# Selective-scan kernel: of every other group of states GpSimd makes both additions, and TensorE adds one product in place of two

## What is computed

```python
dA = jnp.exp(dt_t[..., None] * A)
dBx = dt_t[..., None] * B_t[:, None, :] * x_t[..., None]
h = dA * h + dBx
y = jnp.einsum('bdn,bn->bd', h, C_t)
```

## Time and profile before

| | |
|---|---|
| median of 3 runs | 5212.23 us (5211.99 to 5219.82) |
| the profiled execution | 5224.23 us, its span 5222.4 us |
| TensorE matmuls busy | 4637.5 us, 89% |
| VectorE busy | 4505.1 us, 86% |
| GpSimd busy | 3920.3 us, 75% |
| ScalarE busy | 3588.5 us, 69% |
| mean granted TensorE clock | 0.954 |

### The profile page before, as it was taken

How to read it: one execution, slowest core, us unless ns; L and a number is a source line. 1 busy time by engine, 2 the same in 40 slices (tenths; PEclk the granted TensorE clock), 3 DMA queues, 4 the chain that set the end, 5 groups by cost and what they waited for, 6 DMA issues and landing times.

```text
span 5222.4 us, 73049 instructions
## 1 busy us (share of the span) xinstructions
PE 4637.5 (89%) x22816; PEld 3957.5 (76%) x22816; DVE 4505.1 (86%) x7793; ACT 3588.5 (69%) x8734; POOL 3920.3 (75%) x2218
## 2 busy tenths in 40 slices
PE   5677889989899998989999898999989899998886
PEld 4466777878787787878778787878878787886766
DVE  2598988989899898989989898999989898998950
ACT  2477667777777777777777777777777777776730
POOL 0387777878788787878878787877878787888840
PEclk8788989999999999999999999999999999998998
DMA  4423224343432434343243434324343433433222
GB/s 152 153 83 127 105 89 158 121 156 130 148 132 106 172 115 163 124 153 131 102 172 120 159 123 158 129 102 172 119 161 118 163 123 107 166 106 140 87 94 85
DMA packets 158436, 682.05 MB, mean 131 GB/s; under 512 B 18912, under 2 KB 27744, under 8 KB 108896
## 3 DMA queue, kind: packets, MB, share of 16 engines
q1 hardware_dynamic: 139616, 643.82, 35.0%
q10 hardware_dynamic: 18432, 33.56, 1.7%
HBM read 622.26 MB, written 55.05 MB: 130 GB/s over the span
## 4 chain that ended last, share of the span: by engine, by line
POOL 58%; issue 22%; PE 11%; DVE 4%; DMA 3%; ACT 2%; POOLq 1%; SPq 0%; DVEq 0%; ACTq 0%
POOL dbx L349 36%; POOL half L357 18%; PE gx L521 4%; POOL dtx L392 3%; PE g L554 2%; DVE hb L923 2%; PE g L437 1%; PE ys L447 1%; DMA bb<-bc_scratch 1%; DMA bc_scratch<-ssmT 1%; POOL x L372 1%; DVE gx L977 1%; DVE hc L938 1%; PE gx L486 1%; DMA wf<-wf_scratch 0%
## 5 line engine op out<-in xcount | busy, mean ns | idle before, releaser
L923 DVE TENSOR_TENSOR_SCAN hb<-hb,hstate,dbx 128x256 f32<-128x256 f32 x4096 | 2843.5, 740 | 146.6 <-ACT hb L695 129.4
L349 POOL TENSOR_TENSOR dbx<-dtx,bb 128x1024 f32<-128x1024 f32 x1024 | 2414.8, 2358 | 638.2 <-DVE hb L923 559.0
L695 ACT ACTIVATE hb<-dt,a_neg 128x256 f32<-128x256 f32 x4096 | 1789.1, 468 | 66.4 <-ACT hstate L691 0.2
L357 POOL TENSOR_TENSOR half<-hc 128x512 f32<-128x512 f32 x1024 | 1301.0, 1270 | 286.9 <-DVE hc L938 246.3
L447 PE MATMUL ys<-half,ident 128*128 128x256 f32 x4096 | 1133.0, 401 | 357.7 <-POOL half L357 357.6
L938 DVE TENSOR_TENSOR hc<-hb,cb 128x512 f32<-128x512 f32 x2048 | 1379.2, 673 | 0.0
L447 PEld LDWEIGHTS ys<-half,ident 128*128 128x128 f32 x4096 | 756.2, 195 | 566.4 <-POOL half L357 414.4
L554 PE MATMUL g<-ybuf,wo 128*128 128x256 f32 x4096 | 1019.5, 395 | 24.6 <-DVE ybuf L958 12.0
L521 PE MATMUL gx<-xnT,wx 128*128 128x256 f32 x4096 | 965.9, 391 | 24.8 <-issue 13.4
L537 PE MATMUL ys<-xnT,wz 128*128 128x256 f32 x4096 | 926.7, 379 | 6.8 <-DVE ybuf L958 6.8
L554 PEld LDWEIGHTS g<-ybuf,wo 128*128 128x128 f32 x4096 | 808.9, 199 | 151.1 <-issue 34.3
(11 more groups left out here) (59 smaller groups left out, 2444.3 us busy)
## 6 DMA issues: line engine op xcount, KB each, us to landing
wx<-in_win SPq DMA_DIRECT2D x128, 1024.0 KB, 4.8
wz<-in_win SPq DMA_DIRECT2D x128, 1024.0 KB, 4.8
wo<-in_wout SPq DMA_DIRECT2D x128, 1024.0 KB, 5.0
wf<-wf_scratch SPq DMA_DIRECT2D x128, 512.0 KB, 3.3
xc_scratch<-xcn ACTq DMA_DIRECT2D x128, 256.0 KB, 2.0
xcs<-xc_scratch SPq DMA_DIRECT2D x128, 256.0 KB, 5.1
bb<-bc_scratch SPq DMA_DIRECT2D x64, 512.0 KB, 6.9
cb<-bc_scratch SPq DMA_DIRECT2D x64, 512.0 KB, 6.1
```

Source lines behind the costliest of these rows:

```text
L349: nc.gpsimd.tensor_tensor(dbx[:, k % 2, :].rearrange("p (n t) -> p n t", n=NQ), dtx[:, a * T:(a + 1) * T].unsqueeze(1).to_broadcast([P, NQ ...
L357: nc.gpsimd.tensor_tensor(half[:, k % 4, :], hc[:, k % 2, 0:HALF], hc[:, k % 2, HALF:GW], ALU.add).then_inc(halves, 1)
L695: ins = nc.scalar.activation(h[:, m * T:(m + 1) * T], dt[:, j % 2, a * T:(a + 1) * T], ACT.Exp, scale=a_neg[:, ds((2 * j + a) * N + 2 * v ...
L923: ins = nc.vector.tensor_tensor_scan(h[:, m * T:(m + 1) * T], h[:, m * T:(m + 1) * T], dbx[:, k % 2, (2 * w + m) * T:(2 * w + m + 1) * T], ...
```

## The change

GpSimd's `group_sum` gives the odd groups (k = 1, 3, 5, 7) a second addition: it waits for its own first one, through a new semaphore pair_sums, and adds the second 256 columns of half onto the first 256, in place; only then TensorE is told. TensorE's `group_sum` makes one product for an odd group, of those 256 columns, and two for an even one as before.

```diff
--- before.py
+++ after.py
@@ -204,6 +204,7 @@
         deq_a, deq_b, a_ready = sem("deq_a"), sem("deq_b"), sem("a_ready")
 
         dbxs, halves, dtx_ready, bias_add = sem("dbxs"), sem("halves"), sem("dtx_ready"), sem("bias_add")
+        pair_sums = sem("pair_sums")
         id_zero, id_ready, zeroed = sem("id_zero"), sem("id_ready"), sem("zeroed")
 
         with nc.Block() as first_units:
@@ -354,7 +355,15 @@
             def group_sum(S, k):
                 pool.wait_ge(hcs, after(UNITS * S + 2 * k + 2))
                 pool.wait_ge(sum_mm, after(8 * S + k - 3))
-                nc.gpsimd.tensor_tensor(half[:, k % 4, :], hc[:, k % 2, 0:HALF], hc[:, k % 2, HALF:GW],
+                both = nc.gpsimd.tensor_tensor(half[:, k % 4, :], hc[:, k % 2, 0:HALF], hc[:, k % 2, HALF:GW],
+                                               ALU.add)
+                if k % 2 == 0:
+                    both.then_inc(halves, 1)
+                    return
+
+                both.then_inc(pair_sums, 1)
+                pool.wait_ge(pair_sums, after(4 * S + k // 2 + 1))
+                nc.gpsimd.tensor_tensor(half[:, k % 4, 0:T], half[:, k % 4, 0:T], half[:, k % 4, T:HALF],
                                         ALU.add).then_inc(halves, 1)
 
             def iteration(st, c):
@@ -443,9 +452,9 @@
 
                         a, q = divmod(k, NQ)
                         pe.wait_ge(halves, after(8 * SG + k + 1))
-                        for i in range(2):
+                        for i in range(2 - k % 2):
                             mm = nc.tensor.matmul(ys[a][:, 0:T], ident[:], half[:, k % 4, i * T:(i + 1) * T],
-                                                  start=False, stop=(q == NQ - 1 and i == 1),
+                                                  start=False, stop=(q == NQ - 1),
                                                   skip_group_check=True)
                         mm.then_inc(sum_mm, 1)
 
```

## The result

The changed kernel takes 5380.6 us (median of 4 runs, 5377.4 to 5383.5) against 5213.4 us for the kernel before in the same comparison: ratio 1.032, 95% interval 1.030 to 1.034. It is 3.2% slower, 167 us.

A forecast was written before the change was run, and what follows sets the result against it. A loop of GpSimd's arc and TensorE's arc bounds the kernel. Plain steps +164, steps j=7 and j=0 +23, chunk 0 +8 and chunk 15 +13 sum to +208 us on 5212.2: 5420 us, range 5300 to 5500.

The forecast's parts named there:

- The two arcs: Gate to the start of the last late group (late 7), 16.48 us, GpSimd's; from there to the next gate, 18.98 us, TensorE's.
- c: Cost on GpSimd of one second addition: 0.9 us, 0.68 for the add and 0.21 for waiting for its first.
- TensorE's arc: From late 7 to the next gate, 18.98 us: three products of 0.43 us drop out, −1.29 us.
- the wait for half 0: TensorE reaches group 0 sooner but half 0 is not ready: about 0.34 us of late 7's gain waits there.
- plain step: One of six steps per chunk without norm work, 78 in chunks 2 to 14: 35.46 to 37.6 us, +164 us.
- The fall of the clock: TensorE falls to 1.2 GHz in each plain step, after waiting 3.5 us before late 7; price 1.6 us.
- The signs named ahead: Add 0.73 us; halves 37.6 us apart; TensorE wait 3.5; late 7 doubled; clock near 0.95; VectorE wait 0.5 to 1.3.
- The other steps: Steps j=7 and j=0: +1.8 us per chunk, +23 us; chunk 0 +8, chunk 1 0, chunk 15 +13 us.
- Rival A: The clock holds despite the 3.5 us wait before late 7: plain step 36.3 us, total 5312 us; 14%.
- Rival B: A dear second addition (1.48 us) or a second slow stretch of TensorE: plain step 38.8 us, total 5530 us; 12%.
- C: Faster: TensorE's shorter stream outweighs GpSimd's additions, if c is below 0.645 us; total 5192 us; 4%.
- D: No change: c near 0.645 us at a held clock, or unseen slack on GpSimd's arc; 5212 us; 4%.

The follow-up runs named there:

- the filler: Changed kernel with six products of a blank (zero) matrix on TensorE between late 6 and late 7: 5266.5 us; three such products in the kernel before: 5182.4 us.
- the additions alone: Changed kernel, but TensorE keeps both products for odd groups, so their second half is counted twice: 5567.6 us, ratio 1.068.
- products alone: Kernel before, but TensorE makes one product for each odd group and GpSimd no second addition: 5159.1 us, ratio 0.990.

## Why the prediction was right, and where its sizes were off

- **The two arcs** of the prediction held. Gate to late 7: forecast 16.48 + 1.8, measured 18.08; c was 0.81, not 0.9. The addition was 0.73 us, 0.72 as interpolated before the overlap. The wait for itself was mis-sized: the second addition starts 0.08 us after the end of the first, where I had taken 0.17, the distance of dtx and dbx 0 (with the overlap of 0.04 that is lost, 0.12 and not 0.21). Why dbx 0 starts later is not shown. The Trainium skill, "GPSIMD Engine Reference", Performance versus the Vector engine, gives a rate per element of a two-input operation, from which 0.55 us for 256 elements is an estimate; the row has 0.73. By the rows alone, 1.27 us for 512 and 0.73 for 256, about 0.18 us does not depend on the width (an estimate).
- **TensorE's arc** at full clock: forecast 18.98 − 1.29 + 0.34 for the wait for half 0 = 18.03; measured 18.11, with that wait at 0.34. The plain step without a fall, 36.3 in the prediction, is 36.20. Group 0 starts 3.63 us after late 7, before 3.64: the product that late 7 saves wins nothing.
- **The fall of the clock** came as forecast from the waits in chunks 0, 1 and 15. The wait before late 7 is 3.20 us, forecast 3.5. But its price was taken from chunk 1 by the length at which its steps settled, 1.6 us, and this is the term that was mis-sized: a step with the short fall costs 37.3 − 36.2 = 1.1, and one in six has none. In chunk 1 the clock over a step was 0.91, with the short fall it is 0.95: TensorE is slow for about half as long. The mean price over the 78 steps is 1.05. The new plain step is 37.25 us, not 37.6, and the plain steps cost 139 us, not 164: half of the 50 us by which the sum of 208 exceeds the 158 of the profiled executions. By the medians 5420 was 39 us too high.
- **The signs named ahead.** Late 7 at the doubled duration came in part: 1.20 to 1.22 us in 35 of the 78 plain steps, 0.70 in 28, between in 15. VectorE's wait before the late gate is 0.23 and 0.24 us in the rows, not 0.5 to 1.3.
- **The other steps.** Forecast and measured: the steps to j=7 +1.5 and +1.85 each; the steps to j=0, with the one after them, +0.3 against −0.84 for the steps to j=0 alone; chunk 0 +8 and +3.9; chunk 1 0 and −0.5; chunk 15 +13 and +9.1. Together 44 forecast and 19 measured with all the rest. About 14 us of the gap are at j=0; that the two products saved count in full there is likely but not shown. A part of it is a matter of counting: the step after j=0, which stands among the plain ones, takes 38.27 us on average, 1.2 more than the other five.
- **Rival A** (the clock holds, 5312 us) is what the filler makes of the changed kernel, 5266.5 us, and 13 plain steps of 78 behave so by themselves. **Rival B**'s second slow stretch is there in 11 of 78, and in 35 of the kernel with the additions alone. **C and D** fell with c: 2c = 1.6 us against a gain of 0.87. C's condition in the prediction, 2c < 1.29, was too mild, as it leaves out the 0.34 us for half 0 that the sum counts: by that sum it is 2c < 0.95, and C's own c of 0.54 (0.55 by the slope of the rows) would have made the plain step 0.1 us longer, not 0.21 shorter. The kernel with groups 1 and 3, where the additions are off the arc, shows what a gain takes.
- That the short fall costs 1.1 us in the changed kernel and 1.6 with the additions alone is nearly all the 0.34 us for half 0, which a slow TensorE doesn't wait and which the kernel with the additions alone never waits. What stays open: why the same wait of 3.20 us comes with no fall in 13 steps, a short one in 54 and a long one in 11.

## What to carry to other kernels

Moving work from a busy engine to one with idle time pays, here, only where the idle time is: find for each piece which arc of the loop it lies on, on the engine that gives and on the one that takes. Here the same change on two groups costs 5.3% on groups 5 and 7, whose additions lie ahead of the hand-over to TensorE, and gains 1.5% on groups 1 and 3. And before work is taken from TensorE, look at its longest wait per pass: if that grows, the clock may take a part of the gain back, and filling the wait is worth a try.

## What the runs showed of the hardware that I had not expected

- Useless products in a wait of TensorE made the changed kernel 2.1% faster (5380.6 to 5266.5 us) and the kernel before 0.6%.
- Of TensorE's clock in the plain steps: it fell in 13 of 78 with a longest wait of 1.93 us (products alone), in none of 78 with 1.50 (before; groups 1 and 3), in 65 of 78 with 3.20 (the changed kernel) and in 74 of 78 with 3.10 (additions alone, both products kept on each odd group).
- In all 512 cases of the changed kernel the second addition, which waits for the one just before it on GpSimd, starts 0.08 us after that one's end.
